# Dense feed-forward jobs: lower products with tokens on partitions, gates as per-partition scalars, and three expert jobs between the last feed-forward jobs

## The reference, cut to what matters

```
# end of the layer 0 attention part: an ordinary feed-forward (here: an m job)
x = x + ob @ w_out + b_out
h2 = _ln(x, ln2_g, ln2_b)
m = gelu(h2 @ w1 + b1, approximate=False) @ w2 + b2      # 128 -> 512 -> 128
return x + m

# layer 0 ffn: eight experts, every expert on every token (here: e jobs)
logits = einsum('bld,ed->ble', x, gate_weight)
kth_val = sort(logits.reshape(-1))[B * L * CAPACITY - 1]   # 3072nd smallest of 32768
mask = (logits >= kth_val);  gates = logits * mask
h = gelu(einsum('bld,ehd->bleh', x, w1) + b1, approximate=True)
y = einsum('bleh,edh->blde', h, w2) + b2.T
out = einsum('blde,ble->bld', y, gates)
```

## Time and profile before

| | |
|---|---|
| time, median of 3 runs | 1062.15 us (1059.59 to 1066.69) |
| the profiled execution, first to last instruction | 1062.5 us |
| attention of layer 0 | 0 to 244.5 us |
| dense stage, up to its last norm | 244.5 to 691.0 us |
| PE / DVE / ACT / POOL busy, share of the span | 89% / 81% / 71% / 38% |

### The profile page before, as it was taken

The page is one execution under the profiler, slowest core; times in us unless marked ns, Lnnn a source line. Parts: engine busy times, 40 slices in busy tenths (PEclk is TensorE's granted clock), DMA queues, the critical chain, the costliest instruction groups (busy, mean ns, idle before and its releaser), DMA issues. The chain is left out here.

```text
span 1062.5 us, 28952 instructions
## 1 busy us (share of the span) xinstructions
PE 944.1 (89%) x10222; PEld 607.5 (57%) x10222; DVE 859.6 (81%) x2328; ACT 756.3 (71%) x1476; POOL 405.7 (38%) x568
## 2 busy tenths in 40 slices
PE   5999999994889999999999999678888874899996
PEld 3788888872445444444444444246666653788862
DVE  4988988845888999868899999848888866888854
ACT  2666666645889888888888878346767653688854
POOL 3544444443354100000000000023478867676653
PEclk9999999967899999999999999969999985999998
DMA  8333333000002200032212222010111102232318
GB/s 268 123 107 107 107 106 108 24 3 20 1 6 74 72 1 1 1 104 70 77 71 75 87 66 74 20 53 22 32 52 51 54 27 74 75 86 82 85 45 221
DMA packets 61005, 72.60 MB, mean 68 GB/s; under 512 B 8875, under 2 KB 37805, under 8 KB 60865
## 3 DMA queue, kind: packets, MB, share of 16 engines
q1 hardware_dynamic: 50080, 59.36, 17.9%
q0 software_dynamic: 4544, 8.60, 2.4%
q10 hardware_dynamic: 6240, 2.79, 1.1%
HBM read 40.14 MB, written 31.49 MB: 67 GB/s over the span
## 5 line engine op out<-in xcount | busy, mean ns | idle before, releaser
L808 ACT ACTIVATE d__hf<-d__HB,dense__d 128x512 f32<-128x512 f32 x288 | 184.7, 679 | 39.2 <-PE d__HB L1047 38.2
L867 DVE TENSOR_TENSOR d__hl<-d__hf,d__hh 128x1024 f16<-128x1024 f32 x144 | 173.6, 1219 | 20.4 <-ACT d__hh L813 18.1
L813 ACT ACTIVATE d__hh<-d__hf 128x1024 f16<-128x1024 f32 x144 | 152.2, 1057 | 4.6
L781 POOL TENSOR_SCALAR d__rstd<-d__mv 128x4 f32<-128x4 f32 x16 | 14.2, 886 | 353.6 <-DVE d__mv L990 353.6
L1045 PE MATMUL d__YB<-d__hh,d__w2h 128*128 128x512 f16 x288 | 110.5, 384 | 2.5 <-DVE d__tmp L924 2.5
L1046 PE MATMUL d__HB<-d__xl,d__w1h 128*128 128x512 f16 x288 | 110.9, 385 | 0.0
L1045 PE MATMUL d__HB<-d__xh,d__w1h 128*128 128x512 f16 x288 | 110.8, 385 | 0.0
L1047 PE MATMUL d__HB<-d__xh,d__w1l 128*128 128x512 f16 x288 | 110.6, 384 | 0.0
L316 POOL TENSOR_SCALAR_AFFINE_SELECT a__pt<-a__pt 128x512 f32<-128x512 f32 x128 | 81.3, 657 | 75.4 <-ACT a__pt L364 75.3
L1046 PE MATMUL d__YB<-d__hl,d__w2h 128*128 128x512 f16 x288 | 110.1, 382 | 0.0
L1047 PE MATMUL d__YB<-d__hh,d__w2l 128*128 128x512 f16 x288 | 109.9, 382 | 0.0
(11 more groups left out here) (402 smaller groups left out, 2544.4 us busy)
## 6 DMA issues: line engine op xcount, KB each, us to landing
rows<-a__blank SPq DMA_DIRECT2D x72, 268.0 KB, 3.2
d__G<-gates SPq DMA_DIRECT2D x64, 256.0 KB, 3.2
c__xin<-rows SPq DMA_DIRECT2D x39, 134.0 KB, 2.2
dense__stage<-e_w SPq DMA_DIRECT2D x16, 256.0 KB, 3.1
b__stage<-e_w SPq DMA_DIRECT2D x32, 128.0 KB, 2.2
c__yb<-parts SPq DMA_DIRECT2D x8, 256.0 KB, 8.4
c__yb<-parts ACTq DMA_DIRECT2D x8, 256.0 KB, 8.9
out<-c__xo SPq DMA_DIRECT2D x8, 256.0 KB, 2.3
```

The costliest lines, as they stand in the source:

```text
L808: act.activation(hf[:, q, f], HB[:, f], gelu, scale=1.0 / WS, bias=b1[:, at:at + 1]).then_inc(s_["h_free"], 1)
L813: act.activation(hh[:, j % (LEAD + 1), f - 1:f + 1], hf[:, q, f - 1:f + 1], ACT.Copy).then_inc(s_["hi_done"], 1)
L867: dve.tensor_tensor(hl[:, p, f], hf[:, q, f], hh[:, p, f], ALU.subtract).then_inc(s_["lo%d_done" % i], 1)
```

## The change

- **Lower products.** The three float16 factors change places: hh and hl (128 x 128 pieces of the gelu's output) are now the stationary operand and the weights w2h, w2l the moving one, so that YB has tokens on partitions. 12 matmuls of 512 columns become 48 of 128 columns a job, each with its own weight load. They run in two halves, each behind one `low`.
- **m results.** `accm` and its four transposes go. DVE makes r from YB and xs by one scalar_tensor_tensor. The bias b2 of the feed-forward is added to x beforehand by POOL in the attention stage (`xm_done`, two 128x128 adds in each of 16 steps), from a tile mb2 that one more DMA in ACT's queue loads.
- **Folds.** The gate of a token is a per-partition scalar: a fold is four scalar_tensor_tensor of 128x128 (xa += y * gate) straight into xa. G, its 64 DMAs, tmp and acc go. The bias of the experts comes in at the end of a chunk by one float32 matmul of gates and b2 (32 x 512) into PB in place of the four transposes; it does not wait for the folds. The results put aside are folded one a step in steps 31 to 52.
- **Order of jobs.** The m jobs stand at steps 0, 1, 2, 3, 4, 6, 8, 10; three e jobs of chunk 0 at 5, 7 and 9. The search starts three steps later (13) and ends at 30; folding begins at step 31 as before. Expert weights are split at steps 0, 2, 4, 6, 7, 8, 9, 10.

The core of the diff:

```diff
+M_AT = (0, 1, 2, 3, 4, 6, 8, 10)
+def jobs_0():
+    pairs = ((c, e) for c in range(NC_) for e in range(E))
+    return [("m", M_AT.index(s), 0) if s in M_AT else ("e",) + next(pairs) for s in range(JOBS)]
+COUNT_0 = M_AT[-1] + 3
+KNOWN_0 = COUNT_0 + ROUNDS + 2
+FOLD_0 = KNOWN_0 + 1
+KEPT = [s for s in range(FOLD_0 - 1) if JOB[s][0] == "e"]
+FIRST_OF = [JOB.index(("e", 0, e)) for e in range(E)]
...
 def raw_pair(s):
-    for j in range(M_JOBS, FOLD_0):
-        if kept_raw(j) and FOLD_0 + (j - M_JOBS) * 9 // 5 == s:
-            return j
-    return None
+    i = s - FOLD_0
+    return KEPT[i] if 0 <= i < len(KEPT) else None
...
# attention_0, POOL
+                if what == "shift" and k == 0:
+                    pool.wait_ge(hn_done, n + 1)
+                    pool.wait_ge(xb_done, n + 1)
+                    for a in range(2):
+                        ins = pool.tensor_tensor(x[:, 2 * n + a, :], x[:, 2 * n + a, :], mb2[:], ALU.add)
+                    ins.then_inc(xm_done, 1)
...
# dense_0, SP
-            for k, j in enumerate(order):
-                _, c, e = job(j)
-                wait(sp, s_["g_used"], k - G_RING + 1)
-                sp.dma_start(G[:, k % G_RING], gates[e:e + 1, toks(c)].to_broadcast([P, CT])
-                             ).then_inc(s_["g_in%d" % (k % G_RING)], 16)
...
# dense_0, ACT
-                if 0 <= c < M_JOBS:
-                    act.wait_ge(s_["y_full"], c + 1)
-                    wait(act, s_["pb_full"], left[("post", c - 2)] + 1 if c >= 2 else 0)
-                    act.activation(accm[:, c % 2], YB[:, c % 2], ACT.Identity, scale=1.0 / WS,
-                                   bias=cols[:, 2:3]).then_inc(s_["yf%d" % (c % 2)], 1)
...
# dense_0, DVE
+            def weighed(y, j):
+                _, c, e = JOB[j]
+                for a in range(4):
+                    t = 4 * c + a
+                    ins = dve.scalar_tensor_tensor(out=xa[:, t, :], in0=y[:, a, :],
+                                                   scalar=gates[:, t * E + e:t * E + e + 1], in1=xa[:, t, :],
+                                                   op0=ALU.mult, op1=ALU.add)
+                return ins
             def fold(j):
...
+                dve.wait_ge(s_["counted"], ROUNDS + 3)
+                dve.wait_ge(s_["y_full"], j + 1)
+                dve.wait_ge(s_["y_free"], j)
+                sums.wait()
+                y = YB[:, j % 2].rearrange("p (a c) -> p a c", a=4)
+                weighed(y, j).then_inc(s_["y_free"], 1)
...
# dense_0, PE
             def down(j):
-                for f in range(FB):
-                    if f % 2 == 0:
-                        pe.wait_ge(s_["lo%d_done" % (f // 2)], j + 1)
-                    ins = split_product(YB[:, q], w2h[:, cut], w2l[:, cut], hh[:, p, f], hl[:, p, f], f == 0,
-                                        f == FB - 1)
+                for half_of in range(2):
+                    pe.wait_ge(s_["lo%d_done" % half_of], j + 1)
+                    for a in range(4):
+                        dst, t = YB[:, q, a * P:(a + 1) * P], slice(a * P, (a + 1) * P)
+                        for f in (2 * half_of, 2 * half_of + 1):
+                            at = (weights_of(j) * FB + f) * P
+                            cut = slice(at, at + P)
+                            pe.matmul(dst, hh[:, p, f, t], w2h[:, cut], start=(a == 0 and f == 0), stop=False,
+                                      skip_group_check=True)
+                            pe.matmul(dst, hh[:, p, f, t], w2l[:, cut], start=False, stop=False,
+                                      skip_group_check=True)
+                            ins = pe.matmul(dst, hl[:, p, f, t], w2h[:, cut], start=False, stop=(f == FB - 1),
+                                            skip_group_check=True)
...
-                if s in ended and s != CLOSING:
-                    turned_sum(s)
+                if s + 1 in ended:
+                    c = ended[s + 1]
+                    pe.wait_ge(s_["pb_free"], left[("epost", c)])
+                    pe.wait_ge(s_["b2_done"], 1)
+                    part = slice(32 * (c % 4), 32 * (c % 4) + 32)
+                    pe.matmul(PB[:], gT[part, c // 4], b2[part, :], start=True, stop=True).then_inc(s_["pb_full"], 1)
```

More of the change, by code:

```diff
@@ L589, with m_at, ended_0 @@
 CLOSING = JOBS - 1 - LEAD
-def job(s):
-    return ("m", s, 0) if s < M_JOBS else ("e", (s - M_JOBS) // E, (s - M_JOBS) % E)
+M_AT = (0, 1, 2, 3, 4, 6, 8, 10)
+def jobs_0():
+    pairs = ((c, e) for c in range(NC_) for e in range(E))
+    return [("m", M_AT.index(s), 0) if s in M_AT else ("e",) + next(pairs) for s in range(JOBS)]
+JOB = jobs_0()
+COUNT_0 = M_AT[-1] + 3
[3 more added lines that the diff above has]
+FIRST_OF = [JOB.index(("e", 0, e)) for e in range(E)]
+def m_at(s):
+    return JOB[s][1] if 0 <= s < JOBS and JOB[s][0] == "m" else None
 def is_pair(s):
-    return M_JOBS <= s < JOBS
-def kept_raw(s):
-    return is_pair(s) and s + 1 < FOLD_0
+    return 0 <= s < JOBS and JOB[s][0] == "e"
 def raw_pair(s):
-    for j in range(M_JOBS, FOLD_0):
-        if kept_raw(j) and FOLD_0 + (j - M_JOBS) * 9 // 5 == s:
-            return j
-    return None
-def folds_0():
-    out = []
+    i = s - FOLD_0
+    return KEPT[i] if 0 <= i < len(KEPT) else None
+def ended_0():
+    last = {}
     for s in range(FOLD_0, JOBS + 1):
-        out += [(s, s - 1)]
+        if is_pair(s - 1):
+            last[JOB[s - 1][1]] = s
         if raw_pair(s) is not None:
[L619 to L631, removed]
+            last[JOB[raw_pair(s)][1]] = s
+    return {s + 1: c for c, s in last.items()}
 def uses_0(ended):
@@ L637, in uses_0, with dense_0 @@
     for s in range(BEGIN, END):
[L638 to L646, removed]
+        if s + 1 in ended:
+            left.append(("epost", ended[s + 1]))
+        if m_at(s - 2) is not None:
+            right.append(("turn", m_at(s - 2)))
+            left.append(("logits", m_at(s - 2)))
+        if m_at(s + LEAD + 2) is not None:
+            right.append(("lift", m_at(s + LEAD + 2)))
         if 0 <= s - COUNT_0 <= ROUNDS + 1:
             left.append(("sum", s - COUNT_0))
-        if s == COUNT_0 + ROUNDS + 2:
+        if s == KNOWN_0:
             left.append(("gates", 0))
     return {u: k for k, u in enumerate(left)}, {u: k for k, u in enumerate(right)}
-def dense_0(nc, d, keep, gates, rows, stages):
+def dense_0(nc, d, keep, stages):
     with ExitStack() as ctx:
@@ L668, in dense_0 @@
         hl = m.sb("hl", [P, LEAD + 1, FB, CT], F16)
[L669 to L672, removed]
+        kept = m.sb("kept", [P, NC_, CT])
         half = m.sb("half", [P, 4])
@@ L701, in dense_0 @@
         gt = m.sb("gt", [P, N])
+        gates = m.sb("gates", [P, N])
         gT = m.sb("gT", [P, 2, P])
@@ L728, in weights_of @@
         def weights_of(s):
-            kind, _, e = job(s)
+            kind, _, e = JOB[s]
             return E if kind == "m" else e
         def raw(s):
[L733 to L739, removed]
+            i = KEPT.index(s)
+            v = (kept[:].rearrange("p i (a c) -> p (i a) c", a=4), x1, xs)[i // NC_]
+            return v[:, tiles(i % NC_), :]
         def left_full(eng, *use):
@@ L800, in hidden @@
             def hidden(j):
-                kind, _, e = job(j)
-                gelu = ACT.Gelu if kind == "m" else ACT.Gelu_apprx_tanh
+                gelu = ACT.Gelu if JOB[j][0] == "m" else ACT.Gelu_apprx_tanh
                 q = j % 2
@@ L1049, in hidden @@
             def hidden(j):
-                kind, c, e = job(j)
+                kind, c, e = JOB[j]
                 pe.wait_ge(s_["xl0_done" if kind == "m" else "xl1_done"], c + 1)
@@ L2232, in program @@
             attention_0(nc, d, keep, rows, m1)
-            dense_0(nc, d, keep, gates0, rows, m1)
+            dense_0(nc, d, keep, m1)
         with ExitStack() as c2:
@@ L2327, in layout, with per_tile @@
     down = lambda w: np.ascontiguousarray(w.reshape(-1, FB, P, C).transpose(2, 0, 1, 3).reshape(P, -1))
+    def per_tile(b):
+        z = np.zeros((4, E, 4, C), np.float32)
+        for t in range(4):
+            z[t, :, t] = b
+        return np.tile(z.reshape(4 * E, 4 * C), (4, 1))
     per_row = lambda b: np.ascontiguousarray(b.reshape(-1, P).T)
@@ L2357, in layout @@
     out["c32"] = pack("c32", c)
-    b2 = np.zeros((4, E, 4, C), np.float32)
-    for t in range(4):
-        b2[t, :, t] = a["L1_ffn_b2"]
-    out["e1_b2"] = np.tile(b2.reshape(4 * E, 4 * C), (4, 1))
+    out["e1_b2"] = per_tile(a["L1_ffn_b2"])
     out["gate0"] = np.ascontiguousarray(a["L0_ffn_gate_weight"].T)
```

194 lines of the change are left out of this document (77 added, 117 removed).

## The result

The changed kernel takes 1068.55 us, median of 11 runs (1061.90 to 1072.01), against 1062.15 in this series; the ratio to before is 1.005, 95% interval 1.0029 to 1.0071. Two more series of the same kernel gave 1.0007 (0.998 to 1.0034) and 1.0026 (1.0006 to 1.0047). The mean of the three is 1.0028, about 3 us slower, where 4 us faster were forecast; the second interval, taken alone, includes no change. The profiled execution is the shortest of its eleven (span 1060.2 us); it shows how the stage works, but not the whole loss.

A forecast was written before the change was run, and what follows sets the result against it. No engine alone bounds the dense stage's beginning; from job 13 on PE's instructions do. From the 1062.5 us span, -3.0 (beginning), -2.4 (job 13 to stage end) and +0.5 (hops) gave 1057.6, predicted as 1058; range 1048 to 1069.

The forecast's parts named there:

- Bias matmul: On PE at eight chunk ends: 0.55 us each, 4.4 in all, added to PE's sum from job 13 on.
- Search rounds: On PE from job 13 on: 17 counting rounds of the search at 0.14 us, 2.4 in all.
- End: Behind the last matmul: one fold of 1.15 and 4.74 from r on, with a hop 5.95 us.
- The beginning: First lower product (job 0) to job 13's: job 13 starts 3.0 us earlier; bounds 11.4 earlier and 2.6 later.
- the walk: Beginning, step by step by the longest engine: DVE 8.32 early, ACT 8.0 in steps 3 to 8; job 13 at 369.5.
- +0.5 for hops: Allowance in the final sum for further hops: 0.5 us slower.
- rival 2: Weight loads bound the lower product on PE: +2.03 us a job, time near 1178; chance 0.03.
- F: DVE's time for one fold of four 128x128 operations: between 1.11 and 1.31 us, taken as 1.15.
- PE sum: PE's work in steps 31 to 52: 22 x 5.27 + 5 x 0.53 = 118.6 us, set against DVE's 70.2 + 44F.
- F = 1.22: Steps 31 to 52: fold time up to which PE's one-step lead hides DVE; each 0.1 above costs 4.4 us.
- Rival 1: DVE becomes the bound in steps 31 to 52, F 1.36 to 1.56: 1064 to 1073 us; chance 0.15.
- Rival 3: The order of jobs gives nothing in the beginning: 1063 us, 1061 to 1066 with its neighbours; chance 0.2.

The follow-up runs named there:

- bias_f16: The changed kernel with the float32 bias matmul of a chunk's end as three float16 matmuls of 32x512 (high and low parts); 0.9993 of the time before.
- plain_order: The changed kernel without its order of jobs, the m jobs at steps 0 to 7 and search and folds three steps earlier; 1.0036 of the time before.
- experiment 3: The changed kernel with the tanh gelu for m jobs too, 0.9991 of the time before; ACT's timeline of the changed kernel is shown beside it.
- after_third: The changed kernel run a third time, unaltered; 1.0026 of the time before.
- fold_of_five: The changed kernel with a fifth, unused 128x128 operation in each fold; no ratio given, dense stage 429.7 us against 420.7 in the changed kernel's profiled execution.
- bias_one_pass: The changed kernel with the bias's three float16 products stacked into one 96x512 matmul, gates turned by eight float16 transposes; 0.9952 of the time before.

## Why the prediction failed

It was wrong: 1058 forecast, faster; measured slower, at 1068.55 inside the range of 1048 to 1069.

- **Bias matmul: the step that failed, and the most of it.** The term "8 x 0.55 = 4.4 (two of its form took 1.12)" read the x2 of that row as two matmuls. It is one in float32: seven cost 1.15 each in PE's pace, the eighth hides beside the last fold. 8.1 in place of 4.4, +3.7. A rule of the Trainium skill fits (FP8 and Floating Point Precision, "TensorE Precision Notes"): true float32 takes four passes through PE's array. Four of 0.216 and the 0.2 by which the 32-row form is longer in bias_f16 make an estimated 1.06, near the measured 1.15. The next start in the trace of before, 1.05 behind that row, would have given the price, and line 1612 that the x2 belongs to one matmul.
- **Search rounds.** Taken at 0.14, measured 0.19: some +0.8. **End.** 5.95 forecast behind the last matmul, 6.4 measured: +0.4. With the bias they turn the middle and the end from 316.0 into 321.0 or 321.1, a forecast -2.4 into +2.6.
- **The beginning.** -3.0 forecast; -1.6 without and +0.8 to +1.0 with the further loss of clock. The order itself is worth its 2.7 (plain_order), but the rest of the change costs 1.1 here (102.3 against 101.2). That this is the 0.08 of each lower product, which the walk left out, is likely and was not tried alone. The walk's parts can be read at ACT's gelus of jobs 5 and 11 (292.26 and 342.31, experiment 3) and at job 13: 21.8, 50.1 and 27.8 where it has 21.4, 48.0 and, with its 2 for the clock, 28.8. So steps 3 to 8, put at ACT's 8.0 each, were the part too short, by 2.0, and by 3.8 in after_third. The walk counted a loss of clock as 2 us (its last sum, 367.6 + 2, is 369.6 and not 369.5); the further loss of 2.4 to 2.6 comes in some executions and not in others.
- **Together:** the forecast of -4.9 held +0.5 for hops that no trace shows, so its other terms come to -5.4. With +3.7, +0.8, +0.4 and the beginning's +1.4 to +4.0 that is +0.9 to +3.5; the traces have +1.0 to +3.6.
- **Right:** 5.27 a job and 0.056 between matmuls of 128 columns, so that rival 2 falls. The Trainium skill has 81 ns for this stream (TensorE: Matmul & The Clock Gate, "Back-to-back issue gap"); 2.68 us for 48 say 56. Right too: F (1.15 forecast, 1.12), no wait of PE for DVE in steps 31 to 52, the stand of 4.3 at job 5, eight loads, a gain at the end (3.3), and no visible cost of POOL's adds (the adds that write x1 start 13.41 us apart before and after, in most steps).
- **Right in part by luck:** that DVE never made PE wait. The prediction's PE sum had 0.53 for a chunk end, and the 1.15 that it took gave DVE room. Its point of F = 1.22 becomes 1.29 with 1.15, beside the 1.28 from fold_of_five; with the 0.22 of bias_one_pass it becomes 1.18, and there PE waits 1.8 us at F = 1.12 already. A sum over all 22 steps hides what single steps ask of DVE. Rival 1's 1064 to 1073 holds the measured time, but none of its waits is in the traces of the change.
- **Rival 3** gave 1063 for an order that gives nothing. It comes nearest to the three series, but for another reason: the order gives something, and PE's pace takes it back.
- **What stays open.** The first series measured +0.5%, 5 us; the traces explain 1.0 to 3.6. The rest lies within the spread that starts and attention stages show, and no run separates it.

## What to carry to other kernels

Where an engine is never idle in a stage, price what the change adds to that engine by the distance of the starts of its neighbours, and find out how many records of a trace belong to one instruction before dividing by a count. Moving work off a dense engine (transposes for a bias matmul) helps only if what replaces it is cheaper in its own type: one float32 matmul a chunk in a float16 stream was the difference between a loss and a gain here (1.0026 against 0.9952). And a wait put into the busiest engine can cost more than its length when its clock falls behind it: 3.5 us of wait cost 1.6 more in fold_of_five.

## What the runs showed of the hardware

A matmul of 32 rows among matmuls of 128 rows stood 0.09 to 0.1 off its neighbours on both sides, beside the 0.216 of its length; one of 96 rows (0.22 to the next) did not. A float32 matmul of 32x512 added 1.15 to PE's pace, more than five float16 ones of 128x512 at 0.216 each. A float32 matmul with a 128x128 weight and three columns, the sum of a search round, cost 0.14 behind matmuls of 512 columns and 0.19 behind those of 128.
